# A macaron transformer block on one core: where the first Hadamard stage gets its first batch ready, and where the routed rows of the last two batches are added

## The chip, the cores and the metric

The kernel runs on one core of one Trainium2 chip. The metric is the device time of one execution in microseconds (us). The engines are PE (TensorE), DVE (VectorE), ACT (ScalarE), POOL (GpSimd) and SP (SyncE, which here only issues DMA transfers).

## The reference

The input `x` has 4 batches of 512 tokens with 256 features, all float32. Five layers follow each other, each added to its input:

```
x = x + 0.5 * experts(layernorm(x))          # 8 experts, the best 2 of each token, twice in all
x = x + attention(layernorm(x))              # causal, rotary, 16 heads
x = x + 0.5 * experts(layernorm(x))
x = x + 0.5 * hadamard_ffn(layernorm(x))     # silu(x W1) * (x W3), Walsh-Hadamard transform, W2
x = x + feature_attention(layernorm(x))      # sine and cosine features
x = x + 0.5 * hadamard_ffn(layernorm(x))
```

In the experts layer every token is sent to two experts, and the two results come back weighted by the token's two routing weights. The Hadamard layer's transform is folded into its last weight: `W2` is multiplied with the Hadamard matrix once, ahead of the layer.

## The kernel before

The whole `x` stays in SBUF, as `g.x`: 16 tiles of 128 tokens, 4 tiles to a batch. The program is a chain of stages (`experts_stage` 0, `attention_stage`, `experts_stage` 1, `hadamard_stage` 0, `features_stage`, `hadamard_stage` 1). Each stage is one block in which the five engines run their own hand-written lists in parallel and wait for each other by semaphores. Between two stages stands a barrier of all engines (`Semaphores.clear`, L64 to L66): no engine begins the next stage before all have ended this one and POOL has cleared the stage's semaphores.

float32 products are made of three matmuls of a high and a low part. ACT makes the high part of an operand (a copy to the type float32r) and DVE the low part (the operand less its high part).

**The end of experts stage 1.** The expert units write the results of the routed tokens to the DRAM tensor `made_rows`. Then SP waits until all of it is written and issues eight transfers of 512 KB (L564), for each batch `b` the rows of the first choice and of the second (`r` is 0 or 1). They land in `back`, which has two slots (`b % 2`) in the space of the expert weights `w`: batches 0 and 1 are fetched at once, batches 2 and 3 when their slot has been read. DVE adds them to `g.x` (L1040), one `scalar_tensor_tensor` for each tile and each `r`: 8 instructions for a batch, 32 in all. Meanwhile PE multiplies `W2` with the Hadamard matrix into banks 0 to 3 of PSUM (L726, 128 matmuls), ACT takes its high part (L823), and DVE its low part (L1028), between the adds of batch 1 and of batch 2.

**The start of Hadamard stage 0.** `Norm` is a helper whose methods stand in each engine's list. For a batch, `stats` on DVE takes mean and variance of the 4 tiles (L91, L96); `rstd` on POOL makes the inverse deviation (L119, L122); `normalise` on DVE applies it (L131); `turn` on PE transposes the batch into two banks (L142, 8 transposes); `high` on ACT (L148) and `low` on DVE (L153) split it. Only then can PE start on batch 0.

**The units of Hadamard stage 0.** There are 32 units `n`, 8 (`c`) for each batch `b`. `first(n)` on PE (L1978) is 12 matmuls of 512 columns; ACT's sigmoid (L2031), DVE's `gate` (L2076) and `product` (L2083), ACT's `high` (L2037) and DVE's `low` (L2088) make the hidden part, and `second(n)` on PE (L1990) is 12 matmuls of 256 columns with `W2`. PE runs two units ahead: its list is first(n + 2), second(n). DVE's list in unit `n` is gate(n + 1), low(n), product(n + 1), and then, where the unit has one, a piece of other work: with c = 0 the adding of the batch before to `g.x` (L2095), with c = 1 the statistics of the next batch, with c = 2 its normalising, with c = 4 its split. With c = 3, 5, 6 and 7 there is none.

## Time and profile before

| what | value |
|---|---|
| time, median of 3 runs | 1222.45 us (1217.13 to 1224.24) |
| the profiled execution: its own time | 1228.02 us |
| the profiled execution: its span, from the first to the last instruction | 1226.3 us |
| PE busy, share of the span | 84% |
| DVE busy, share of the span | 60% |
| mean granted TensorE clock | 0.899 of full speed |

The profiled execution is one execution, and its time of 1228.02 us lies 5.6 us above the median. The span leaves out 1.7 us around the instructions. All durations are read from this execution. The rows of a timeline give the start in us from the beginning of the span, the duration in us, the engine, the line of the kernel and the instruction, how many of them are merged in the row (x), and in square brackets how long the engine was idle before and what released it.

### The profile page before, as it was taken

How to read it: one execution, taken by the hardware profiler on the slowest of the kernel's cores; microseconds unless marked ns; L12 is line 12 of the kernel's file. 1: busy time of each engine (PE TensorE's matmuls, PEld its weight loads, DVE VectorE, ACT ScalarE, POOL GpSimd, SP SyncE). 2: the span in 40 equal slices, each digit the busy share in tenths (PEclk: the TensorE clock that was granted, in tenths of full speed). 3: DMA queues.
4: the chain of work that ended last, by engine and by line, in shares of the span. 5: the costliest groups of instructions: out<-in, count | busy, mean ns of one | idle time of the engine just before them, and what ended most of it. 6: DMA issues, size and time to landing. Idle time of an engine off the chain costs nothing. (4 is left out here: it accounts for less than half of the span.)

```text
span 1226.3 us, 18054 instructions
## 1 busy us (share of the span) xinstructions
PE 1024.6 (84%) x6181; PEld 833.7 (68%) x6181; DVE 736.9 (60%) x1754; ACT 463.2 (38%) x806; POOL 438.6 (36%) x474
## 2 busy tenths in 40 slices
PE   4459996469999999952889893999988998789997
PEld 3348775346566665542678782888878988678886
DVE  5754342786777878537344326565657777656553
ACT  3314332226666765514233320322334443222222
POOL 2036664335363622202365630000109889400000
PEclk9579999667999998875899996999997999999999
DMA  9043222400000001118352233000010030000000
GB/s 338 8 159 100 82 82 79 135 1 1 2 1 19 1 18 35 36 34 328 92 201 82 79 117 112 1 1 1 1 69 1 1 69 1 1 1 18 18 12 24
DMA packets 36878, 72.34 MB, mean 59 GB/s; under 512 B 8180, under 2 KB 25654, under 8 KB 36536
## 3 DMA queue, kind: packets, MB, share of 16 engines
q1 hardware_dynamic: 29112, 50.21, 12.3%
q0 software_dynamic: 7680, 20.98, 5.2%
q8 instruction: 54, 0.88, 0.3%
q14 instruction: 32, 0.26, 0.1%
HBM read 47.04 MB, written 24.13 MB: 58 GB/s over the span
## 5 line engine op out<-in xcount | busy, mean ns | idle before, releaser
L1978 PE MATMUL ps<-xt,w 128*128 128x512 f32 x768 | 192.9, 402 | 5.6 <-PEq L66 3.2
L1978 PEld LDWEIGHTS ps<-xt,w 128*128 128x128 f32 x768 | 143.4, 193 | 35.8 <-DVE xt L153 6.2
L1680 DVE CUSTOM_DVE_ANT_0 ps<-ps,att_mask 128x128 f32<-128x128 f32 (+3 forms) x256 | 119.2, 517 | 39.2 <-PE ps L1295 39.0
L680 PE MATMUL ps<-moe_w,moe_narrow_xb 128*128 x480 | 127.8, 402 | 0.0
L119 POOL TENSOR_TENSOR var_eps<-bn,eps 128x4 f32<-128x4 f32 x24 | 5.2, 217 | 319.8 <-DVE bn L96 292.4
L2076 DVE TENSOR_TENSOR had_gated<-ps,had_sig 128x512 f32<-128x512 f32 x64 | 44.3, 692 | 119.8 <-ACT had_sig L2031 119.8
L590 POOL DMA_INDIRECT moe_xs<-xn_rows,moe_index x80 | 80.6, 1008 | 97.4 <-DVE moe_index L962 52.5
L596 POOL DMA_INDIRECT made_rows<-moe_units_made,moe_index x80 | 81.6, 1020 | 92.8 <-ACT moe_units_made L800 76.9
L981 DVE TENSOR_TENSOR moe_narrow_xb<-ps,moe_narrow_xb 128x512 fp32r<-128x512 f32 x40 | 27.7, 692 | 140.7 <-ACT moe_narrow_xb L782 94.7
L2031 ACT ACTIVATE had_sig<-ps 128x512 f32<-128x512 f32 x64 | 38.2, 597 | 186.4 <-PE ps L1978 186.4
L680 PEld LDWEIGHTS ps<-moe_w,moe_narrow_xb 128*128 128x128 f32 x480 | 92.2, 192 | 19.6
L1546 ACT ACTIVATE att_early_probs<-ps 128x384 f32<-128x384 f32 (+1 forms) x192 | 90.7, 527 | 28.7 <-PE ps L1310 27.7
L1990 PE MATMUL ps<-w,had_yhi 128*128 128x256 f32 x512 | 94.6, 283 | 1.8 <-DVE had_ylo L2088 1.8
L1197 POOL TENSOR_SCALAR_AFFINE_SELECT att_early_probs<-att_early_probs 128x256 f32<-128x256 f32 x128 | 53.6, 432 | 116.5 <-ACT att_early_probs L1546 116.4
L1990 PEld LDWEIGHTS ps<-w,had_yhi 128*128 128x128 f32 x512 | 83.4, 190 | 7.8 <-DVE had_ylo L2088 2.6
L782 ACT ACTIVATE moe_narrow_xb<-ps 128x512 fp32r<-128x512 f32 x40 | 23.9, 598 | 143.5 <-PE ps L664 125.7
L1295 PE MATMUL ps<-att_kt,att_q 48*128 48x256 f32 (+3 forms) x256 | 66.8, 424 | 11.0 <-DVE att_q_stack L1680 8.3
L1990 PE MATMUL ps<-w,had_ylo 128*128 128x256 f32 x256 | 72.4, 283 | 0.0
L2210 POOL TENSOR_TENSOR fea_inv_norm<-fea_norm,neg_half 128x24 f32<-128x24 f32 x16 | 66.7, 4172 | 11.3 <-DVE fea_norm L2437 11.1
L2290 PE MATMUL ps<-fea_wv_prod,ident 128*128 128x256 f32 x256 | 63.3, 405 | 7.4 <-DVE fea_wv_prod L2479 7.4
L706 PE MATMUL ps<-moe_w,moe_units_yb 128*128 x480 | 69.4, 284 | 0.0
L706 PEld LDWEIGHTS ps<-moe_w,moe_units_yb 128*128 128x128 f32 x480 | 63.5, 192 | 0.1
(274 smaller groups left out, 2230.0 us busy)
## 6 DMA issues: line engine op xcount, KB each, us to landing
moe_w<-in_moe SPq DMA_DIRECT2D x16, 768.0 KB, 8.5
back<-made_rows SPq DMA_DIRECT2D x8, 512.0 KB, 5.4
x<-x_turned SPq DMA_DIRECT2D x8, 512.0 KB, 7.6
moe_w<-made_rows SPq DMA_DIRECT2D x8, 512.0 KB, 4.7
low_weights<-moe_w SPq DMA_DIRECT2D x4, 768.0 KB
moe_w<-low_weights SPq DMA_DIRECT2D x4, 768.0 KB, 16.7
x<-in_x SPq DMA_DIRECT2D x4, 512.0 KB, 5.1
xn_rows<-moe_wide_xn SPq DMA_DIRECT2D x4, 512.0 KB, 9.2
```

Of the source, the lines that this page charges most:

```text
L590: nc.gpsimd.indirect_dma_start(out=xs[:, j % 2, i, :], out_offset=None, in_=g.xn_dram[:, :], in_offset=at(0, 2 * j + i)).then_inc(gathered ...
L596: nc.gpsimd.indirect_dma_start(out=g.made_dram[:, :], out_offset=at(1, 2 * j + i), in_=made[:, j % 2, i, :], in_offset=None) \
L680: last = nc.tensor.matmul(h_bank(j, i), xb[a][:, j % 2, i, k, :], weight(c), start=False, stop=(k == KC - 1 and c == 1))
L706: last = nc.tensor.matmul(O_BANK[:, i * D:(i + 1) * D], yb[a][:, j % 2, i, c, :], weight(q), start=False, stop=(c == IC - 1 and q == 1), s ...
L1197: last = nc.gpsimd.affine_select(block, block, [[0, 2], [1, P]], ALU.is_ge, 0.0, base=0, channel_multiplier=-1)
L1295: last = nc.tensor.matmul(g.ps[:, a, col:col + n], q1[at, w % 2, i * P:n], kt[at, w % 4, 0:n], start=True, stop=True)
L1546: nc.scalar.activation(probs[:, w % 3, a, at:at + n], g.ps[:, 2 + a, 0:n], ACT.Exp, scale=HD ** -0.5).then_inc(exp_done, 1)
L1680: last = nc.vector.tensor_tensor_reduce(g.ps[:, a, col:col + n], g.ps[:, a, col:col + n], mask[:, SEQ - n:SEQ], -1.0, 3.0e38, ALU.add, ALU ...
L1978: last = nc.tensor.matmul(g.ps[:, bank(n, half), :], w[a][:, k, c * P:(c + 1) * P], xt[low][:, b % 2, k, :], start=(k == 0 and q == 0), st ...
L1990: last = nc.tensor.matmul(o, a[:, n % 4, at], g.w2[w][:, c, :], start=(c == 0 and q == 0 and i % 2 == 0), stop=(c == HC - 1 and q == 2), s ...
L2210: nc.gpsimd.tensor_tensor(inv_norm[:, t % 4, :], norm2[:, t % 4, :], g.neg_half[:, 0:QKH], ALU.pow) \
L2290: last = nc.tensor.matmul(g.ps[:, 5 + t % 2, 0:D], g.ident[:, :], wv_prod[:, t % 2, k, :, :].rearrange("p h d -> p (h d)"), start=(k == 0) ...
```

## The change

Batch 0 of Hadamard stage 0 is added, normalised, transposed and split at the end of experts stage 1, ahead of the barrier. In detail:

- `f.xn`, `f.xt` and `f.back` get fixed places in SBUF where the expert weights were; `f.back` has three slots instead of two, and it stays alive into the Hadamard stage. SP so issues six transfers at once (batches 0, 1 and 2) and those of batch 3 after batch 0 has been added.
- DVE adds batches 0 and 1 at the end of the experts stage. Batches 2 and 3 are added within the Hadamard units, four instructions each after the product of the units (b, c) = (0, 3), (0, 5), (0, 7) and (1, 3).
- `stats`, `rstd`, `normalise`, `turn`, `high` and `low` of batch 0 stand in the experts stage (`f.first_norm`). The transposes go to banks 0 and 1, and the product of `W2` and the Hadamard matrix goes to banks 4 to 7 instead of 0 to 3.
- The low part of `W2` is made by DVE at the start of the Hadamard stage, and PE waits for it (`f.w2_low`) ahead of second(0).
- The statistics of the next batch wait until that batch has been added (`f.combined`).

```diff
-            experts_stage(nc, g, ins, 0, x_dram)
+            experts_stage(nc, g, ins, 0, x_dram, None)
...
+        f = Shared()
+        f.base = nc.sbuf_base
+        f.xn = nc.alloc_sbuf_tensor_at("xn", [P, 2, BT, D], F32, offset=f.base)
+        f.xt = [nc.alloc_sbuf_tensor_at(f"xt{q}", [P, 2, KC, SEQ], F32R, offset=f.base + (q + 1) * 8192) for q in range(2)]
+        f.back = nc.alloc_sbuf_tensor_at("back1", [P, 3, 2, BT, D], F32, offset=f.base + 42 * 1024)
+        f.back_here = [sem(f"back1_here{s}") for s in range(3)]
+        f.combined, f.w2_low = sem("combined1"), sem("w2_low")
+        f.first_norm = Norm(nc, sem, g, "had0_norm", 2, f.xn)
+        experts_stage(nc, g, ins, 1, None, f)
...
+def add_rows(nc, g, f, dve, b, r):
+
+    if r == 0:
+        dve.wait_ge(f.back_here[b % 3], 32 * (b // 3 + 1))
+    else:
+        dve.wait_ge(f.combined, 2 * b + 1)
+    for i in range(BT):
+        t = b * BT + i
+        last = nc.vector.scalar_tensor_tensor(out=g.x[:, t, :], in0=f.back[:, b % 3, r, i, :],
+                                              scalar=g.route[:, r, t:t + 1], in1=g.x[:, t, :],
+                                              op0=ALU.mult, op1=ALU.add)
+    last.then_inc(f.combined, 1)
...
# experts stage 1, SP
-                if b >= 2:
-                    sp.wait_ge(combined, 2 * (b - 1))
+                if b >= 3:
+                    sp.wait_ge(f.combined, 2 * (b - 2))
# POOL
+            if which == 1:
+                f.first_norm.rstd(pool, 0)
# PE
                 for o in range(HC):
+                    if o == HC - 2:
+                        pe.wait_ge(out_done, PAIRS)
...
-                            last = nc.tensor.matmul(g.ps[:, o // 2, (o % 2) * D:(o % 2 + 1) * D], had_r[:, odd, :],
+                            last = nc.tensor.matmul(g.ps[:, 4 + o // 2, (o % 2) * D:(o % 2 + 1) * D], had_r[:, odd, :],
...
+                f.first_norm.turn(pe, 0, 0)
# ACT
+                f.first_norm.high(act, 0, 0, f.xt[0][:, 0, :, :])
# DVE
-            for b in range(BATCH if which == 1 else 0):
...
+                add_rows(nc, g, f, dve, 0, 0)
+                add_rows(nc, g, f, dve, 0, 1)
+                dve.wait_ge(f.combined, 2)
+                f.first_norm.stats(dve, 0, x_block(0))
+                add_rows(nc, g, f, dve, 1, 0)
+                f.first_norm.normalise(dve, 0, x_block(0))
+                add_rows(nc, g, f, dve, 1, 1)
+                f.first_norm.low(dve, 0, 0, f.xt[0][:, 0, :, :], f.xt[1][:, 0, :, :])
+                dve.wait_ge(w2_hi, 1)
...
# Hadamard stage
+        LATE = {(0, 3): (2, 0), (0, 5): (2, 1), (0, 7): (3, 0), (1, 3): (3, 1)}
...
+                if n == 0 and which == 0:
+                    pe.wait_ge(f.w2_low, 1)
...
-                norm.stats(dve, 0, x_block(0))
-                norm.normalise(dve, 0, x_block(0))
-                norm.low(dve, 0, pair(0), xt[0][:, 0, :, :], xt[1][:, 0, :, :])
+                nc.vector.scalar_tensor_tensor(
+                    out=g.w2[1][:, :, :].rearrange("p a n -> p (a n)"),
+                    in0=g.ps[:, 4:8, :].rearrange("p a n -> p (a n)"), scalar=HID ** -0.5,
+                    in1=f32(g.w2[0][:, :, :]).rearrange("p a n -> p (a n)"), op0=ALU.mult, op1=ALU.subtract) \
+                    .then_inc(f.w2_low, 1)
...
+                if which == 0 and (b, c) in LATE:
+                    add_rows(nc, g, f, dve, *LATE[b, c])
                 if c == 1 and b + 1 < BATCH:
+                    if which == 0:
+                        dve.wait_ge(f.combined, 2 * b + 4)
                     norm.stats(dve, b + 1, x_block(b + 1))
```

The first place is DVE's list from the low part of `W3` (L1024 before, L1048 now) to the first gate of the Hadamard stage (L2076 before, L2094 now); the two branches between are the end of one stage and the start of the next. The instructions of before:

```order
L1024 TENSOR_TENSOR w_1_8891<-moe_w_raw,w_0_8890 128x2048
L1040 SCALAR_TENSOR_TENSOR x<-moe_w,moe_route_back,x 128x256 x16
L1028 SCALAR_TENSOR_TENSOR w_1_8893<-ps,w_0_8892 128x2048
L1040 SCALAR_TENSOR_TENSOR x<-moe_w,moe_route_back,x 128x256 x16
L373 UNCONDITIONAL_BRANCH
L2069 UNCONDITIONAL_BRANCH
L91 BN_STATS bn<-x 128x6 x4
L96 BN_AGGR bn<-bn 128x2 x4
L131 TENSOR_SCALAR xn<-x,bn,rstd 128x256 x4
L153 TENSOR_TENSOR xt<-ps,xt 128x1024
L2076 TENSOR_TENSOR had_gated<-ps,had_sig 128x512
```

And the same stretch of the change, in which L387 is the add of the routed rows:

```order
L1048 TENSOR_TENSOR w_1_8891<-moe_w_raw,w_0_8890 128x2048
L387 SCALAR_TENSOR_TENSOR x<-back_8897,route,x 128x256 x8
L94 BN_STATS bn<-x 128x6 x4
L99 BN_AGGR bn<-bn 128x2 x4
L387 SCALAR_TENSOR_TENSOR x<-back_8897,route,x 128x256 x4
L134 TENSOR_SCALAR xn<-x,bn,rstd 128x256 x4
L387 SCALAR_TENSOR_TENSOR x<-back_8897,route,x 128x256 x4
L156 TENSOR_TENSOR xt_8896<-ps,xt_8895 128x1024
L396 UNCONDITIONAL_BRANCH
L2087 UNCONDITIONAL_BRANCH
L2119 SCALAR_TENSOR_TENSOR w_1_8893<-ps,w_0_8892 128x2048
L2094 TENSOR_TENSOR had_gated<-ps,had_sig 128x512
```

Statistics, normalising and split of batch 0 have moved from behind the barrier to ahead of it, 16 of the 32 adds are gone from this stretch, and the low part of `W2` (L1028, now L2119) has moved behind the barrier.

The second place is DVE's list in the units n = 2 to 5 of the change, from the normalising of batch 1 on (L2094 is the gate, L2106 the low part, L2101 the product):

```order
L134 TENSOR_SCALAR xn<-x,bn,rstd 128x256 x4
L2094 TENSOR_TENSOR had_gated<-ps,had_sig 128x512
L2106 TENSOR_TENSOR had_ylo<-had_y,had_yhi 128x512
L2101 TENSOR_TENSOR had_y<-ps,had_gated 128x512
L387 SCALAR_TENSOR_TENSOR x<-back_8897,route,x 128x256 x4
L2094 TENSOR_TENSOR had_gated<-ps,had_sig 128x512
L2106 TENSOR_TENSOR had_ylo<-had_y,had_yhi 128x512
L2101 TENSOR_TENSOR had_y<-ps,had_gated 128x512
L156 TENSOR_TENSOR xt_8896<-ps,xt_8895 128x1024
```

The four adds stand between the product of one unit and the gate of the next, where before stood nothing; the same holds for the three other places.

The third place is PE's list from the last matmuls of `W2` (L748) to the first of the Hadamard stage (L1998):

```order
L748 MATMUL ps<-moe_wide_part_8910,moe_units_had_r 128x256 x8
L748 MATMUL ps<-moe_wide_part_8911,moe_units_had_r 128x256 x8
L145 MATMUL ps<-ident,xn 128x128 x8
L396 UNCONDITIONAL_BRANCH
L1981 UNCONDITIONAL_BRANCH
L1998 MATMUL ps<-xt_8895,w_0 128x512
```

The eight transposes of batch 0 (L145; before, L142 stood behind the two branches) now end PE's list of the experts stage, so that the first matmul after the barrier is one of `first(0)`.

## Rows read from the trace of the kernel before

**Rows 1.** The page: busy time by engine, share of the span, instructions.
```profile
PE 1024.6 (84%) x6181; PEld 833.7 (68%) x6181; DVE 736.9 (60%) x1754; ACT 463.2 (38%) x806; POOL 438.6 (36%) x474
```

**Rows 2.** Timeline of all engines, 724 to 773 us.
```profile
724.33 15.51 PE L726 MATMUL ps<-moe_wide_part,moe_units_had_r 128*128 128x256 f32 x128
...
736.55 6.67 DVE L1040 SCALAR_TENSOR_TENSOR x<-moe_w,moe_route_back,x 128x256 f32<-128x256 f32 x16 [7.28 <-DMA moe_w<-made_rows]
739.88 1.88 ACT L823 ACTIVATE w<-ps 128x2048 fp32r<-128x2048 f32 x1 [12.94 <-PE ps L726]
743.14 2.28 DVE L1028 SCALAR_TENSOR_TENSOR w<-ps,w 128x2048 fp32r<-128x2048 f32 x1
745.34 6.66 DVE L1040 SCALAR_TENSOR_TENSOR x<-moe_w,moe_route_back,x 128x256 f32<-128x256 f32 x16
...
753.23 1.41 DVE L91 BATCH_NORM_STATS2 bn<-x 128x6 f32<-128x256 f32 x4 [1.23 <-PEq L66]
...
754.75 0.38 DVE L96 BATCH_NORM_AGGREGATE bn<-bn 128x2 f32<-128x6 f32 x4
...
755.49 1.05 POOL L122 TENSOR_TENSOR rstd<-var_eps,neg_half 128x4 f32<-128x4 f32 x1
...
756.57 1.39 DVE L131 TENSOR_SCALAR xn<-x,bn,rstd 128x256 f32<-128x256 f32 x4 [1.44 <-POOL rstd L122]
...
758.02 1.97 PE L142 MATMUL ps<-ident,xn 128*128 128x128 f32 x8 [18.18 <-DVE xn L131]
...
760.02 1.02 ACT L148 ACTIVATE xt<-ps 128x1024 fp32r<-128x1024 f32 x1 [18.27 <-PE ps L142]
...
761.08 1.23 DVE L153 TENSOR_TENSOR xt<-ps,xt 128x1024 fp32r<-128x1024 f32 x1 [3.12 <-ACT xt L148]
...
762.36 10.70 PE L1978 MATMUL ps<-xt,w 128*128 128x512 f32 x36 [2.37 <-DVE xt L153]
```

**Rows 3.** Line L66, 750 to 754 us: the barrier's release of PE.
```profile
L66 PEldq EVENT_SEMAPHORE  x1: 51/51/51, 753.1 to 753.1; - x1
```

**Rows 4.** Timeline of DVE, 782 to 798 us: gates behind units 3 and 5.
```profile
787.27 0.69 DVE L2076 TENSOR_TENSOR had_gated<-ps,had_sig 128x512 f32<-128x512 f32 x1 [3.20 <-ACT had_sig L2031]
...
795.72 0.69 DVE L2076 TENSOR_TENSOR had_gated<-ps,had_sig 128x512 f32<-128x512 f32 x1 [2.33 <-ACT had_sig L2031]
```

**Rows 5.** Windows: us, busy time of each engine, PEclk (granted clock), DMA share, GB/s.
```profile
742.90:758.00 15.10, 0.00 (x0) 0.00 (x0) 12.21 (x30) 0.00 (x0) 2.47 (x8) 0.50 0.53 180
762.36:766.90 4.54, 4.54 (x11) 3.57 (x12) 0.00 (x0) 0.00 (x0) 0.00 (x0) 0.50 0.03 1
773.00:860.00 87.00, 87.00 (x506) 76.46 (x505) 52.81 (x107) 25.43 (x43) 4.37 (x7) 1.00 0.00 1
```

**Rows 6.** DMA issues of 729.0 to 729.5, 729.5 to 730.0 and 730.6 to 731.2 us.
```profile
moe_w<-made_rows SPq DMA_DIRECT2D x1, 512.0 KB, 4.2
...
moe_w<-made_rows SPq DMA_DIRECT2D x1, 512.0 KB, 7.0
...
moe_w<-made_rows SPq DMA_DIRECT2D x1, 512.0 KB, 8.5
```

**Rows 7.** One window inside that burst, columns as in rows 5.
```profile
734.00:735.00 1.00, 1.00 (x10) 1.00 (x9) 0.00 (x0) 0.00 (x0) 0.00 (x0) 1.00 1.02 397
```

**Rows 8.** Timeline of DVE and POOL, 812 to 814 and 882 to 888 us.
```profile
812.43 1.04 POOL L122 TENSOR_TENSOR rstd<-var_eps,neg_half 128x4 f32<-128x4 f32 x1
...
813.20 0.68 DVE L2088 TENSOR_TENSOR had_ylo<-had_y,had_yhi 128x512 fp32r<-128x512 f32 x1
...
882.67 2.75 POOL L1959 TENSOR_TENSOR lqkv<-had_lqkv_raw,lqkv 128x1024 fp32r<-128x1024 f32 x1
...
883.67 3.86 DVE L131 TENSOR_SCALAR xn<-x,bn,rstd 128x256 f32<-128x256 f32 x4
```

**Rows 9.** Windows at the start of Hadamard stage 1, columns as in rows 5.
```profile
1076.29:1079.50 3.21, 0.00 (x0) 0.03 (x1) 1.67 (x2) 1.06 (x2) 0.00 (x0) 1.00 0.00 0
...
1080.94:1084.15 3.21, 3.21 (x9) 2.44 (x8) 0.00 (x0) 0.31 (x1) 0.00 (x0) 0.50 0.00 0
```

More of the change, by code:

```diff
@@ L69, with __init__ @@
 class Norm:
-    def __init__(self, nc, sem, g, tag, slots):
-        self.nc, self.g, self.slots = nc, g, slots
+    def __init__(self, nc, sem, g, tag, slots, rows=None):
+        self.nc, self.g, self.slots, self.rows = nc, g, slots, rows
         s = lambda n: sem(f"{tag}_{n}")
@@ L83, in __init__, with xn @@
         self.lo_done = s("lo_done")
+    def xn(self):
+        return self.g.xn if self.rows is None else self.rows
     def slot(self, b):
@@ L111, in normalise_tiles @@
         for i in tiles:
-            last = nc.vector.tensor_scalar(g.xn[:, q, i, :], x_block(i), g.bn2[:, q, i, 0:1],
+            last = nc.vector.tensor_scalar(self.xn()[:, q, i, :], x_block(i), g.bn2[:, q, i, 0:1],
                                            g.rstd[:, q, i:i + 1], ALU.subtract, ALU.mult)
@@ L130, in normalise @@
         for i in range(BT):
-            last = nc.vector.tensor_scalar(g.xn[:, q, i, :], x_block(i), g.bn2[:, q, i, 0:1],
+            last = nc.vector.tensor_scalar(self.xn()[:, q, i, :], x_block(i), g.bn2[:, q, i, 0:1],
                                            g.rstd[:, q, i:i + 1], ALU.subtract, ALU.mult)
@@ L283, in program @@
         g.lout = upper(ctx, "lout", [P, KC, D])
-        f = Shared()
-        f.xn = sb("xn", [P, 2, BT, D])
-        f.xt = [sb(f"xt{q}", [P, 2, KC, SEQ], F32R) for q in range(2)]
+        sb("front_space", [P, 24 * 256])
         f.bias = sb("bias", [P, 3])
@@ L367, in constants, with experts_stage @@
     nc.gpsimd.tensor_tensor(g.row_e[:, :], g.row_e[:, :], g.row[:, :], ALU.add).then_inc(done, 1)
-def experts_stage(nc, g, ins, which, x_dram):
+def add_rows(nc, g, f, dve, b, r):
[9 more added lines that the diff above has]
+    last.then_inc(f.combined, 1)
+def experts_stage(nc, g, ins, which, x_dram, f):
     with ExitStack() as ctx:
@@ L382, in experts_stage @@
             route_rows = sb("route_rows", [2 * TILES, P])
[L383 removed]
+            route_back = g.route
         b1_all = sb("b1_all", [P, E, 2 * IC])
@@ L397, in experts_stage @@
         xs = sb("xs", [P, 2, 2, D])
-        back = f32(w[0][:, :, :]).rearrange("p e n -> p (e n)")[:, 0:4 * BT * D] \
-            .rearrange("p (s r t d) -> p s r t d", s=2, r=2, t=BT)
         units = Region(nc, ctx, f"{tag}_units", 20480)
@@ L461, in experts_stage @@
         yhi_done, ylo_done, o_ready, out_done = sem("yhi_done"), sem("ylo_done"), sem("o_ready"), sem("out_done")
-        back_here = [sem(f"back_here{s}") for s in range(2)]
-        combined = sem("combined")
         if which == 0:
@@ L563, in _ @@
                     mine = by_sixteens(rows)[:, b * BT:(b + 1) * BT, :]
-                    sp.dma_start(back[:, b % 2, r, :, :], mine).then_inc(back_here[b % 2], 16)
+                    sp.dma_start(f.back[:, b % 3, r, :, :], mine).then_inc(f.back_here[b % 3], 16)
         @block.gpsimd
@@ L1024, in _ @@
                 nc.vector.tensor_tensor(g.w3[1][:, :, :], w3_raw[:, :, :], f32(g.w3[0][:, :, :]), ALU.subtract)
-            for b in range(BATCH if which == 1 else 0):
-                if b == 2:
-                    dve.wait_ge(w2_hi, 1)
-                    nc.vector.scalar_tensor_tensor(
-                        out=flat(g.w2[1][:, :, :]), in0=flat(g.ps[:, 0:4, :]), scalar=HID ** -0.5,
-                        in1=f32(flat(g.w2[0][:, :, :])), op0=ALU.mult, op1=ALU.subtract)
-                dve.wait_ge(back_here[b % 2], 32 * (b // 2 + 1))
-                dve.wait_ge(x_here[b], 16)
-                if b == 0:
-                    dve.wait_ge(route_here, 16)
-                for r in range(2):
-                    if r:
-                        dve.wait_ge(combined, 2 * b + 1)
-                    for i in range(BT):
-                        t = b * BT + i
-                        last = nc.vector.scalar_tensor_tensor(
-                            out=g.x[:, t, :], in0=back[:, b % 2, r, i, :], scalar=route_back[:, r, t:t + 1],
-                            in1=g.x[:, t, :], op0=ALU.mult, op1=ALU.add)
-                    last.then_inc(combined, 1)
+                for b in range(BATCH):
+                    dve.wait_ge(x_here[b], 16)
+                dve.wait_ge(route_here, 16)
+                add_rows(nc, g, f, dve, 0, 0)
[7 more added lines that the diff above has]
+                dve.wait_ge(w2_hi, 1)
 def attention_stage(nc, g, ins):
@@ L1891, in hadamard_stage @@
         yhi_done, ylo_done, second_done, x_added = sem("yhi_done"), sem("ylo_done"), sem("second_done"), sem("x_added")
-        norm = Norm(nc, sem, g, "norm", 2) if which == 0 else f.next_norm
+        norm = f.first_norm if which == 0 else f.next_norm
         BLOCKS = P // HD
         UNITS = HC * BATCH
+        LATE = {(0, 3): (2, 0), (0, 5): (2, 1), (0, 7): (3, 0), (1, 3): (3, 1)}
         x_block = x_of(g)
@@ L2006, in turn_tables @@
                 last.then_inc(f.tables_ps, 1)
-            if which == 0:
-                turn(0)
             first(0)
@@ L2037, in high @@
                 nc.scalar.activation(yhi[:, n % 4, :], y[:, n % 2, :], ACT.Copy).then_inc(yhi_done, 1)
-            if which == 0:
-                norm.high(act, 0, pair(0), xt[0][:, 0, :, :])
             sigmoid(0)
@@ L2114, in _ @@
                     add(b - 1)
+                if which == 0 and (b, c) in LATE:
+                    add_rows(nc, g, f, dve, *LATE[b, c])
                 if c == 1 and b + 1 < BATCH:
+                    if which == 0:
+                        dve.wait_ge(f.combined, 2 * b + 4)
                     norm.stats(dve, b + 1, x_block(b + 1))
```

9 lines of the change are left out of this document (4 added, 5 removed).

## The prediction

> **What bounds the kernel now.** I read the page first: PE is busy 84% of the span, more than any other engine [rows 1]. So a stretch in which PE stands still is where time can be won. The timeline shows one between the two stages [rows 2]. PE's last matmul of the `W2` product ends at 724.33 + 15.51 = 739.84 us, and its first matmul of the Hadamard stage starts at 762.36 us: 22.5 us in which PE does eight transposes (1.97 us) and nothing else. In the same rows the reader can follow what PE waits for. DVE waits until 736.55 us for the routed rows, adds 16 tiles (6.67 us), makes the low part of `W2` (2.28 us), adds 16 more (6.66 us) and ends at 745.34 + 6.66 = 752.00 us. Then come the barrier (DVE starts again at 753.23 us), statistics (to 754.75 + 0.38 = 755.13 us), POOL's inverse deviation, normalising (to 757.96 us), transposes, high part and low part (to 762.31 us), one after the other. The chain begins with the landing of the rows, and it is DVE's from there to 757.96 us, but for the barrier and POOL.
>
> In the units behind it PE is the bound. From 773 to 860 us it is busy 87.00 of 87.00 us [rows 5], and DVE waits in every unit for the sigmoid, 2.33 us ahead of a gate behind a unit without other work, and 3.20 us behind the unit c = 3, in which PE transposes [rows 4]. The two gates there stand two units apart, so a unit lasts (795.72 - 787.27) / 2 = 4.22 us.
>
> **The change part by part.** I take the distance from DVE's first add to PE's first matmul, 762.36 - 736.55 = 25.81 us, and build it again in the new order. One add takes 6.67 / 16 = 0.417 us.
>
> 1. Adds of batch 0, eight: 3.33 us.
> 2. Statistics, from the first to the end of the last, 755.13 - 753.23 = 1.90 us.
> 3. Adds of batch 1, first choice, four: 1.67 us. Before, DVE waited from 755.13 to 756.57 us, 1.44 us, for POOL [rows 2]; that wait now lies under these adds. POOL has issued its last scatter long before, so nothing is ahead of it in its queue.
> 4. Normalising: 1.39 us.
> 5. From its end to the end of the low part, 762.31 - 757.96 = 4.35 us, the same three steps on the same engines. The other four adds of batch 1 (1.67 us) lie under the transposes, since the low part waits for ACT anyway. ACT is free: its high part of `W2` ends at 739.88 + 1.88 = 741.76 us. PE stood at half clock for these transposes before (0.50 from 742.90 to 758.00 us [rows 5]); in the new order they come some 5 us after PE's last matmul, and I take them at half clock again.
> 6. The barrier: from DVE's end to PE's release, 753.1 + 0.05 - 752.00 = 1.15 us [rows 3]. The first matmul needs nothing else then.
>
> The sum is 3.33 + 1.90 + 1.67 + 1.39 + 4.35 + 1.15 = 13.79 us, against 25.81 us: **12.0 us less**. It splits into 16 adds gone from the stretch and four under the transposes (20 x 0.417 = 8.3 us), the low part of `W2` (745.34 - 743.14 = 2.2 us as its part of DVE's time), and POOL's 1.4 us.
>
> What was moved must lie somewhere. The low part of `W2` (2.28 us) now opens DVE's list behind the barrier. Its cover is `first(0)`: the first gate needs PE's twelve matmuls, and `second(0)`, which waits for it, came only behind the 36 matmuls of 10.70 us [rows 2]. Without that cover it would cost 2.28 us. The 16 adds of batches 2 and 3 come in four pieces of 4 x 0.417 = 1.67 us. Behind unit 3, and behind unit 11 in the same position, DVE had 3.20 us free; behind units 5 and 7 it had 2.33 us [rows 4]. So 1.5 and 0.7 us are left over, the gates are not late, and I cost the adds at nothing. If the gaps were not free they would cost up to 4 x 1.67 = 6.7 us. The statistics of batches 2 and 3 wait for adds that stand several units ahead in DVE's own list: nothing.
>
> The transfers: SP now issues six at once. In the burst of four, the first landed after 4.2 us, the second, which batch 0 also needs, after 7.0 us and the last after 8.5 us [rows 6]. They landed in their order, so two more behind them should not delay batch 0: nothing. The bound from the other side is that all share the bandwidth evenly; then two more transfers, 1.05 MB at 397 GB/s [rows 7], make batch 0 late by 2.6 us. Batch 3 is issued when batch 0 is added, as batch 2 was, and needed behind unit 7, over 40 us later. The wait of PE for the last expert output stands ahead of the last quarter of the `W2` product, long after that output: nothing.
>
> The clock: before, PE ran the first 4.54 us behind the wait at half clock [rows 5]. In the new order it has been idle for 3.5 us after the transposes and is at half clock already, so I take the same 4.54 us again. Between nothing gained and half of it, 2.3 us, I choose nothing, since the row nearest to it had eight transposes 2.4 us ahead of it as well.
>
> DVE against POOL: POOL can hold DVE. While POOL ran one `tensor_tensor` of 2.75 us from 882.67 us, four normalisations took 3.86 us [rows 8], where they otherwise take 1.39 us [rows 2]. In the new order the inverse deviation falls on the adds of batch 1. But for this pair the nearest row says nothing happens: the inverse deviation ran from 812.43 to 813.47 us, and a DVE instruction with two inputs from SBUF, as an add has, started at 813.20 us and took its usual 0.68 us [rows 8]. I take nothing, and the bound is POOL's whole part, 756.54 - 755.13 = 1.4 us. The Trainium skill says otherwise (SBUF — State Buffer, section "Who interferes with whom"): a DVE instruction with two SBUF inputs contends with a GpSimd instruction that reads SBUF, and whoever comes second is blocked for the whole of the other. By it the adds and POOL's part would follow one another, and the gain would be 10.6 us.
>
> From the profiled execution's own time of 1228.02 us that leaves 1216.0 us. This execution lies 5.6 us above the median of the runs, 1222.45 us; in the same proportion the median goes to 1222.45 x 1216.0 / 1228.02 = **1210.5 us**.
>
> **The rivals.**
> - *POOL and DVE block each other* over the adds of batch 1. For it speaks the 3.86 us, against it the 0.68 us [rows 8]. It gives 1210.5 + 1.4 = 1211.9 us. Chance 0.10.
> - *Six transfers share the bandwidth* and batch 0 is late. Against it speaks the order of landing [rows 6], for it that the second took 2.8 us longer than the first. 1210.5 + 2.6 = 1213.1 us. Chance 0.10. By the Trainium skill (DMA: Bandwidth & Descriptors, section "Queues, rings and completion order") each DMA engine takes the descriptors of one queue in ring order, which would leave batch 0 where it is.
> - *The late adds reach PE*, because a product or a gate comes late and the two units of lead are used up. Against it speak 0.7 us left in the tightest gap. Wholly exposed they cost 6.7 us: 1217.2 us; half of them 1213.9 us. Chance 0.12.
> - *Slower: PE's clock stays low.* PE enters the stage at half clock, and a unit of 4.22 us then takes up to twice as long. The gain is used up when the half clock holds for 12.0 / 4.22 = 2.8 units longer than before, and the kernel is slower by over 0.5% from 4.3 units on: 1228.6 us or more. Against it: after 15 us of idleness the full clock came back within 4.54 us [rows 5], and after 3.21 us of idleness at the start of the other Hadamard stage half clock held 3.21 us [rows 9]. Chance 0.02.
>
> **How the numbers follow.** The forecast has a chance of 0.62, and 0.04 is left for what I don't see. 1210.5 us is the likeliest. Its own range is 1208 (the half clock saved) to 1213 us (a transfer late). The three runs of before lie from 5.3 us under to 1.8 us over their median, so a median of few runs can be off by some 3 us: I go down to 1205 and, to take in the late adds, up to 1217 us. Within 0.5% (about what a measurement of this kernel can tell from no change) would be above 1216.3 us: there stand half of the late adds' case and little else, 0.07. Slower by over 0.5% is the clock's case, 0.02. Faster: 0.91.
>
> **What would show it.** In the profile of the changed kernel: PE's gap between the `W2` product and the Hadamard stage should be 10.5 us instead of 22.5, with the transposes some 5 us into it; the normalising should start within 0.1 us of the last of four adds (if 1.4 us later, it is POOL); the first add should again come about 7.3 us after the low part of `W3` (if 2.6 us more, the transfers share); the gates behind the late adds should still be released by the sigmoid, with 1.5 and 0.7 us of idleness; and PE should be busy without a break from the first unit on, at full clock after some 4.5 us. The prediction is wrong if PE's first matmul starts later than 752 us, if gates are released by DVE's own adds, or if the low clock lasts longer.

## The result and the profile after

| kernel | median of its runs | runs | ratio to the kernel before, with its interval |
|---|---|---|---|
| before | 1221.38 us (1217.1 to 1224.72) | 6 | |
| changed | 1202.14 us (1198.86 to 1209.8) | 6 | 0.9875 (0.9845 to 0.9906) |

The kernel became faster, by 1.2%. The forecast's ratio was 1210.5 / 1222.45 = 0.990, which lies inside the interval. The profiled execution of the change took 1209.8 us, 18.2 us less than that of before. Only part of this is the change's, and the profile tells which.

The timeline of all engines from the end of experts stage 1 on, in the changed kernel (columns as in rows 2; here and below, `...` stands where rows are left out):

```profile
713.74 13.48 PE L748 MATMUL ps<-moe_wide_part,moe_units_had_r 128*128 128x256 f32 x111
...
716.56 10.98 SPq L582 DMA_DIRECT2D back<-made_rows  x8
723.33 3.38 DVE L387 SCALAR_TENSOR_TENSOR x<-back,route,x 128x256 f32<-128x256 f32 x8 [6.70 <-DMA back<-made_rows]
726.75 1.41 DVE L94 BATCH_NORM_STATS2 bn<-x 128x6 f32<-128x256 f32 x4
...
728.55 1.64 DVE L387 SCALAR_TENSOR_TENSOR x<-back,route,x 128x256 f32<-128x256 f32 x4
...
729.14 1.17 POOL L125 TENSOR_TENSOR rstd<-var_eps,neg_half 128x4 f32<-128x4 f32 x1
730.34 1.38 DVE L134 TENSOR_SCALAR xn<-x,bn,rstd 128x256 f32<-128x256 f32 x4 [0.15 <-POOL rstd L125]
731.64 1.67 DVE L387 SCALAR_TENSOR_TENSOR x<-back,route,x 128x256 f32<-128x256 f32 x4
731.78 1.97 PE L145 MATMUL ps<-ident,xn 128*128 128x128 f32 x8 [4.56 <-DVE xn L134]
733.79 1.02 ACT L151 ACTIVATE xt<-ps 128x1024 fp32r<-128x1024 f32 x1 [4.65 <-PE ps L145]
734.84 1.22 DVE L156 TENSOR_TENSOR xt<-ps,xt 128x1024 fp32r<-128x1024 f32 x1 [1.53 <-ACT xt L151]
...
738.40 11.08 PE L1998 MATMUL ps<-xt,w 128*128 128x512 f32 x36 [4.65 <-PEq L66]
738.41 2.29 DVE L2119 SCALAR_TENSOR_TENSOR w<-ps,w 128x2048 fp32r<-128x2048 f32 x1 [2.35 <-PEq L66]
```

From DVE's first add to PE's first matmul of the Hadamard stage, which I call the seam from here on, it is 738.40 - 723.33 = 15.07 us, against 25.81 us before [rows 2]: 10.7 us less, where the forecast had 12.0. Step by step, forecast and read:

| step | forecast | read |
|---|---|---|
| adds of batch 0 | 3.33 | 726.75 - 723.33 = 3.42 |
| statistics | 1.90 | 728.55 - 726.75 = 1.80 |
| four adds of batch 1 | 1.67 | 1.64, and 0.15 waiting for POOL |
| normalising | 1.39 | 1.38 |
| from there to the end of the low part | 4.35 | 736.06 - 731.72 = 4.34 |
| barrier | 1.15 | 738.40 - 736.06 = 2.34 |

Every step but the last is right within 0.15 us. (The forecast's 1.15 us ends with PE's release by the barrier; in this profile the first matmul starts 0.05 us behind that release.) Of the barrier, the view of one line shows POOL's part (L396 is the end of the stage's block; columns: count, shortest/median/longest ns, first and last start; the last start of each row is the one in this seam):

```profile
L396 DVEq DRAIN  x2: 799/916/1033, 196.4 to 735.1; - x2
...
L396 POOLq DRAIN  x2: 7821/8450/9078, 201.9 to 729.1; - x2
...
L396 PEldq EVENT_SEMAPHORE  x2: 51/51/51, 211.1 to 737.1; - x2
```

and the same line of the kernel before (L373 there):

```profile
L373 DVEq DRAIN  x2: 799/1250/1702, 202.0 to 750.4; - x2
...
L373 POOLq DRAIN  x2: 9077/9082/9088, 207.5 to 725.2; - x2
```

A drain is the instruction with which an engine's queue makes sure at a stage's end that all its work is done. DVE's ends at 735.1 + 1.03 = 736.1 us, but POOL's, begun at 729.1 us, takes 7.82 us, to 736.9 us, and only then is the barrier passed. Before, POOL's drain took 9.08 us from 725.2 to 734.3 us, and DVE was the last, at 752.1 us. In both kernels POOL's drain ends 6.6 us behind POOL's last instruction: before, behind the last scatter, which ended at 727.65 us; in the change, behind the inverse deviation, which ended at 730.31 us and stands near the end of the stage.

The units. The timeline of DVE behind units 3 and 5 (answers to rows 4):

```profile
760.39 1.66 DVE L387 SCALAR_TENSOR_TENSOR x<-back,route,x 128x256 f32<-128x256 f32 x4
763.69 0.69 DVE L2094 TENSOR_TENSOR had_gated<-ps,had_sig 128x512 f32<-128x512 f32 x1 [1.63 <-ACT had_sig L2051]
...
769.72 1.66 DVE L387 SCALAR_TENSOR_TENSOR x<-back,route,x 128x256 f32<-128x256 f32 x4
772.14 0.69 DVE L2094 TENSOR_TENSOR had_gated<-ps,had_sig 128x512 f32<-128x512 f32 x1 [0.76 <-ACT had_sig L2051]
```

The gates are still released by the sigmoid, with 1.63 and 0.76 us of idleness left (forecast: 1.5 and 0.7). From the first matmul to the end of the stage (the release behind the next barrier) it is 146.6 us, before 146.4 us. The granted clock (windows, columns as in rows 5):

```profile
727.20:730.30 3.10, 0.02 (x1) 0.00 (x0) 2.89 (x11) 1.88 (x1) 1.50 (x2) 0.98 0.86 299
730.30:738.40 8.10, 1.97 (x8) 1.59 (x9) 4.19 (x9) 1.02 (x1) 0.04 (x2) 0.50 0.04 18
738.40:742.90 4.50, 4.50 (x11) 3.53 (x12) 2.29 (x1) 0.00 (x0) 1.12 (x6) 0.50 0.78 245
742.90:749.00 6.10, 6.10 (x26) 4.94 (x25) 3.03 (x5) 1.72 (x3) 0.00 (x0) 0.92 0.08 15
```

PE starts the stage at half clock (1.2 GHz). The 0.92 over the next 6.10 us leaves (1 - 0.92) x 6.10 x 2 = 1.0 us more at half clock, so full clock (2.4 GHz) is back after some 5.5 us, where the forecast took 4.54 us [rows 5]. The first 36 matmuls took 11.08 us, before 10.70 us.

**Where the other 7.5 us of the two profiled executions are.** The barrier rows of each profile give the length of every stage. Experts stage 0 took 212.1 us instead of 217.8, experts stage 1 up to the first add 174.7 us instead of 182.0, the features stage 176.1 us instead of 170.6; attention, the units of Hadamard stage 0 and Hadamard stage 1 differ by 0.3 us at most. Together: 5.7 + 7.3 + 10.7 - 5.5 = 18.2 us, of which 10.7 us is the seam. The code of the other three is the same in both kernels, but for the places of some buffers and one wait of PE in experts stage 1. What they depend on is the question of the repeats below.

### The profile page after: what moved, and what is told of

Its sections match the earlier page's. It is cut to its first block and busy times, and to the rows that moved or that the text cites. A ratio compares the mean times of both kernels' runs of the same rounds, so it can differ in the third digit from the quotient of the medians.

```text
span 1208.1 us, 18055 instructions
## 1 busy us (share of the span) xinstructions
PE 1027.2 (85%) x6181; PEld 838.5 (69%) x6181; DVE 734.9 (61%) x1754; ACT 463.0 (38%) x806; POOL 437.2 (36%) x474
## 5 line engine op out<-in xcount | busy, mean ns | idle before, releaser
L1998 PE MATMUL ps<-xt,w 128*128 128x512 f32 x768 | 193.1, 402 | 7.9 <-PEq L66 7.9
L1998 PEld LDWEIGHTS ps<-xt,w 128*128 128x128 f32 x768 | 143.7, 193 | 38.0 <-issue 5.0
L2094 DVE TENSOR_TENSOR had_gated<-ps,had_sig 128x512 f32<-128x512 f32 x64 | 44.2, 691 | 111.5 <-ACT had_sig L2051 111.5
L2314 PE MATMUL ps<-fea_wv_prod,ident 128*128 128x256 f32 x256 | 60.0, 390 | 9.1 <-DVE fea_wv_prod L2503 9.1
```

The costliest lines, as they stand in the source:

```text
L1998: last = nc.tensor.matmul(g.ps[:, bank(n, half), :], w[a][:, k, c * P:(c + 1) * P], xt[low][:, b % 2, k, :], start=(k == 0 and q == 0), st ...
L2314: last = nc.tensor.matmul(g.ps[:, 5 + t % 2, 0:D], g.ident[:, :], wv_prod[:, t % 2, k, :, :].rearrange("p h d -> p (h d)"), start=(k == 0) ...
```

## The experiments

**Theory A**: the change acts at the seam alone, through what it takes off the chain there, and the late adds cost nothing. **Theory B**: it does something more (the other 7.5 us). For the missing 1.2 us at the seam, **theory P**: POOL's drain is long because of the indirect transfers that POOL issued earlier and never drained, and its end moves back when POOL gets an instruction late; **theory Q**: 6 to 7 us behind the last instruction is what a drain of POOL takes in any case.

**1. Both kernels again**, unchanged, on one chip.

> The kernel before, unchanged, once more. Between the two profiled executions so far, stages with the same code differed: experts stage 0 took 217.8 us in one and 212.1 us in the other, the units of experts stage 1 some 7 us less, the features stage 170.6 and 176.2 us. Theory A (these differences belong to the execution, not to the change): this profile differs from the first one of before by several us in these stages, while the distance from the first routed add to the first matmul of the Hadamard stage is again 25.8 us within 0.2 us. Theory B (they come with the change): the stages take 217.8, 336.7 and 170.6 us within 1 us again. The ratio to before is 1.000 within 0.004 under both.

> The changed kernel, unchanged, once more. Theory A (only the seam between the stages gives time, the rest varies by execution): first routed add to first matmul 15.1 us within 0.2 us, the other stages anywhere between the two profiles so far, and a ratio of (1221.4 - 10.7) / 1221.4 = 0.991 within 0.003. Theory B (the change also shortens the experts stages): experts stage 0 again some 212 us, and a ratio of 0.984 to 0.988.

Measured: before 1217.72 us (10 runs), ratio 0.9996 (0.9959 to 1.0033); the change 1208.89 us (6 runs), ratio 0.9886 (0.9848 to 0.9925). Seams 25.80 and 15.07 us. Experts stage 0 took 211.9 and 212.8 us, experts stage 1 to the first add 175.3 and 176.0 us. So in these two profiles the experts stages have the same lengths within 1 us, and the 13.0 us by which they differed in the first pair are not the change's.

**2. The early preparation without the late adds.** The adds of batches 2 and 3 go back to the end of the experts stage, behind the low part of batch 0. The low part of `W2` stays behind the barrier, as in the change.

```diff
+                for b in (2, 3):
+                    for r in range(2):
+                        add_rows(nc, g, f, dve, b, r)
...
-        LATE = {(0, 3): (2, 0), (0, 5): (2, 1), (0, 7): (3, 0), (1, 3): (3, 1)}
+        LATE = {}
```

> Batch 0 is prepared ahead of the barrier as in the change, but batches 2 and 3 are also added there, behind the low part of batch 0. The 16 adds (6.67 us) stand on DVE at the end of the stage, and POOL's drain is over by then: first routed add to first matmul 15.07 + 6.67 - (2.31 - 1.15) = 20.6 us, that is 5.2 us less than before and 5.5 more than the change. If the late adds of the change were in truth partly exposed in the units, the units from first matmul to the stage's end would here be shorter than the 146.5 us of the changed kernel; I expect 146.2 to 146.5 us.

Measured: 1216.18 us (9 runs), ratio 0.9957 (0.9914 to 0.9999); seam 20.83 us, 5.0 us less than before. The 16 adds (6.66 us) stand ahead of the barrier again and cost 20.83 - 15.07 = 5.8 us: they also cover POOL's drain. DVE ends 1.52 us ahead of PE's first matmul here. Of the 5.0 us, 2.2 us belong to the low part of `W2`, which this kernel has off the chain too. From the first matmul to the end of the stage it took 146.8 us, not less than in the change (146.1 to 146.6 us in its three profiles), so the late adds were not partly exposed there.

**3. The late adds alone**, with the low part of `W2` behind the barrier; all six steps of batch 0's preparation go back to the Hadamard stage.

```diff
-                f.first_norm.rstd(pool, 0)
...
-                f.first_norm.turn(pe, 0, 0)
...
-                f.first_norm.high(act, 0, 0, f.xt[0][:, 0, :, :])
...
-                f.first_norm.stats(dve, 0, x_block(0))
...
-                f.first_norm.normalise(dve, 0, x_block(0))
...
-                f.first_norm.low(dve, 0, 0, f.xt[0][:, 0, :, :], f.xt[1][:, 0, :, :])
```

> Batches 2 and 3 are added within the units and the low part of W2 is made behind the barrier as in the change, but batch 0 is normalised, transposed and split behind the barrier as before. First routed add to first matmul: 6.67 (16 adds) + 1.2 (barrier, POOL's drain long over) + 1.90 + 1.44 + 1.39 + 4.35 = 17.0 us, 8.8 us less than before and 1.9 more than the change. So most of the gain would be the work taken out of DVE's list, little the place of the barrier. If the place of the barrier mattered more, this would be above 18 us.

Measured: 1208.09 us (4 runs), ratio 0.9886 (0.9831 to 0.9941); seam 16.98 us, 8.8 us less than before. The timeline of this kernel:

```profile
726.90 6.67 DVE L387 SCALAR_TENSOR_TENSOR x<-back,route,x 128x256 f32<-128x256 f32 x16 [6.58 <-DMA back<-made_rows]
...
738.10 1.38 DVE L134 TENSOR_SCALAR xn<-x,bn,rstd 128x256 f32<-128x256 f32 x4 [1.44 <-POOL rstd L125]
739.41 2.28 DVE L2118 SCALAR_TENSOR_TENSOR w<-ps,w 128x2048 fp32r<-128x2048 f32 x1
...
743.88 10.21 PE L1991 MATMUL ps<-xt,w 128*128 128x512 f32 x36 [2.37 <-DVE xt L156]
```

The low part of `W2` lies under the transposes here, and POOL's 1.44 us are back. So most of the gain needs none of the early preparation: taking 16 adds and the low part of `W2` off the chain is worth 8.8 us. The preparation adds 16.98 - 15.07 = 1.9 us to that. The 5.0 us of (2) and these 8.8 us both hold the 2.2 us of `W2`'s low part, so they don't add up to 10.7 us; and with the late adds gone from the chain, POOL's drain takes back part of what the preparation gives. The ratio of this kernel, 0.9886, is that of the change in (1): the totals don't show the 1.9 us, the seams do.

**4. POOL drained early** (P against Q): a drain in POOL's idle time, ahead of the inverse deviation.

```diff
             if which == 1:
+                nc.gpsimd.drain()
                 f.first_norm.rstd(pool, 0)
```

> The changed kernel with one more instruction: POOL drains right behind its last scatter, while it waits for the statistics anyway (13.7 us idle). In the changed kernel POOL's drain at the end of the stage ends 6.6 us behind the inverse deviation and 0.87 us behind DVE's last instruction, so it is what holds the barrier. Theory P (the 6.6 us belong to the indirect transfers not yet drained): with the drain ahead, the one at the end is short, DVE ends the stage, the barrier takes 1.2 instead of 2.3 us, and first routed add to first matmul is 14.0 to 14.2 us. Theory Q (any POOL work late in this stage costs 6.6 us at its end): 15.1 us as in the change, or more.

Measured: seam 14.40 us (forecast: 14.0 to 14.2); a single run of 1219.8 us, so its total says nothing. The new drain (L625), in the view of its line:

```profile
L625 POOLq DRAIN  x1: 9079/9079/9079, 730.2 to 730.2; - x1
```

the one at the end, in the view of that line:

```profile
L396 POOLq DRAIN  x2: 1272/5180/9088, 208.0 to 746.4; - x2
```

and the timeline up to the first matmul:

```profile
752.16 1.22 DVE L156 TENSOR_TENSOR xt<-ps,xt 128x1024 fp32r<-128x1024 f32 x1 [1.53 <-ACT xt L151]
...
755.04 2.47 PE L1999 MATMUL ps<-xt,w 128*128 128x512 f32 x5 [3.98 <-PEq L66]
```

The 9.08 us are now spent at 730.2 us, where POOL has nothing to do, and they too end 6.6 us behind the last scatter (to 732.63 us); the drain at the end takes 1.27 us instead of 7.82, and DVE is the last at the barrier again. P holds, Q falls: the long drain belongs to something that one drain settles. (The 1.27 us hold the inverse deviation itself: the drain's record begins at 746.4 us, when the 1.17 us of that instruction begin, and ends at 747.7 us, as they do within 0.1 us.) That the something is the indirect transfers fits: in Hadamard stage 0 of the kernel before, which has none, POOL's last instruction ended at 885.38 + 1.35 = 886.7 us and its drain, of 5.12 us from 881.7 us, at 886.8 us. But no run took the transfers away, so it is argued. The seam gets 0.67 us shorter. The barrier's remaining 755.04 - 753.38 = 1.66 us is 0.5 us more than the 1.15 us that I had read off the kernel before. The views of the barrier's own lines show where, first before:

```profile
L65 POOLq EVENT_SEMAPHORE_RANGE_CLEAR  x1: 437/437/437, 752.5 to 752.5; - x1
...
L66 POOLq EVENT_SEMAPHORE  x2: 17/17/17, 753.0 to 753.1; - x2
```

and in the kernel with POOL drained:

```profile
L65 POOLq EVENT_SEMAPHORE_RANGE_CLEAR  x1: 417/417/417, 753.8 to 753.8; - x1
...
L66 POOLq EVENT_SEMAPHORE  x2: 17/17/17, 754.8 to 754.9; - x2
```

Before, POOL passed the barrier on 753.0 - 752.9 = 0.1 us after it had cleared the semaphores; here it took 754.8 - 754.2 = 0.6 us. In the change it took 0.4 us, and in (3), where POOL has no instruction behind its last scatter either, 0.1 us as before. Why POOL is slower there no run isolates.

**5. All 16 late adds in one gap**, that behind unit 5, where DVE has 2.33 us free [rows 4]: the rival of the late adds, made to happen.

```diff
-        LATE = {(0, 3): (2, 0), (0, 5): (2, 1), (0, 7): (3, 0), (1, 3): (3, 1)}
+        LATE = {(0, 5): ((2, 0), (2, 1), (3, 0), (3, 1))}
```

> The changed kernel, but all 16 late adds in one place, behind unit 5: 6.67 us in a gap of 2.33 us, so the next gate is 4.3 us late. The low part behind it was ready 2.1 us before PE wanted it and the product 2.9 us before, so PE should stand still for some 2.2 us once, and first matmul to the end of the stage should be 148.5 instead of 146.4 us. If the lead of PE doesn't count (a late gate stops PE at once), it is 150.7 us; if DVE's time there is free whatever is put in, 146.4 us.

Measured, in a single run of 1223.09 us: seam 15.08 us, from the first matmul to the stage's end 150.1 us instead of 146.4: 3.7 us more, where 2.1 us was expected. Its timeline of PE:

```profile
787.72 2.94 PE L1998 MATMUL ps<-xt,w 128*128 128x512 f32 x12
792.63 0.80 PE L2012 MATMUL ps<-w,had_yhi 128*128 128x256 f32 x2 [1.97 <-DVE had_ylo L2106]
```

and windows at the same place (columns as in rows 5):

```profile
790.66:792.63 1.97, 0.00 (x1) 0.00 (x0) 1.97 (x5) 0.60 (x1) 0.00 (x0) 1.00 0.00 0
792.63:795.36 2.73, 2.73 (x12) 2.73 (x13) 2.44 (x4) 0.63 (x1) 0.00 (x0) 0.50 0.01 3
795.36:798.47 3.11, 3.11 (x14) 2.54 (x13) 0.00 (x0) 0.00 (x0) 0.00 (x0) 0.89 0.00 0
```

The adds take 6.67 us, 4.3 us more than the gap; the lead of two units hides 2.4 us of it, and PE stands still for 1.97 us. After that its clock is at half for 2.73 us and at 0.89 for 3.11 us more, which costs 2.73 x 0.50 + 3.11 x 0.11 = 1.7 us. 1.97 + 1.7 = 3.7 us: a wait of PE costs nearly twice its length here. The length of the wait was forecast well (2.2 us); the cost in clock was left out of the forecast.

**6. PE kept busy** with 32 matmuls of 256 columns between the `W2` product and the transposes and 20 behind them, whose results nobody reads, so that it might arrive at full clock.

```diff
+                def keep_busy(count):
+                    for _ in range(count):
+                        nc.tensor.matmul(g.ps[:, 3, 0:D], had_r[:, 0, :], part[0][:, 0, :], start=True, stop=True)
+                keep_busy(32)
                 f.first_norm.turn(pe, 0, 0)
+                keep_busy(20)
```

> The changed kernel with idle work on PE in the seam: 32 matmuls of 256 columns into an unused bank ahead of the transposes of batch 0 and 20 behind them; nothing reads them. In the changed kernel PE is idle for 4.6 us, transposes at half clock (1.97 us), is idle again for 4.6 us and runs the first 4.5 us of the stage at half clock. If the idleness is what costs the clock, the transposes take 1.04 us and the first 36 matmuls about 8.5 instead of 11.1 us: first add to first matmul 14.3 us (less 0.2 to 0.9 if the drain holds), and first matmul to the end of the stage 144.0 instead of 146.4 us. If the clock falls regardless, all stays as in the change.

Measured: 1224.62 us (10 runs; before on this chip 1233.85 us), ratio 0.9929 (0.99 to 0.9958). Seam 15.08 us, unchanged: the transposes took 1.09 us instead of 1.97, but POOL's drain held the barrier all the same. The expected 14.3 us was missed. PE stood still for 3.15 us ahead of its first matmul, and its clock was 0.71 over the first 5.0 us of the stage. From the first matmul to the end it took 145.4 us, 1.0 us less than the change's 146.4 us; but the kernel of (4), without these matmuls, took 145.6 us, because full clock was back after 3.15 us there. So this one profile does not show that the 1.0 us is the edit's.

**7. Both: POOL drained and PE kept busy.**

> Both edits together, POOL's early drain and PE kept busy. Under theory P and with the clock held: first add to first matmul 13.1 to 13.4 us, first matmul to the end of the stage 144.0 us, together 4.0 to 4.5 us less than the change; ratio to before about 0.991 less 0.0035 = 0.988, within 0.004.

Measured: 1222.59 us (6 runs), ratio 0.9884 (0.9841 to 0.9928). Seam 13.58 us and 144.1 us to the end, together 157.7 us; the change has 15.07 + 146.3 = 161.4 us there (146.3 us is the mean of its three profiles). That is 3.7 us less, where 4.0 to 4.5 us was expected. The same kernel was run again with the change beside it (8); its timeline of PE there:

```profile
751.50 1.10 PE L145 MATMUL ps<-ident,xn 128*128 128x128 f32 x8 [0.67 <-DVE xn L134]
752.35 2.63 PE L755 MATMUL ps<-moe_wide_part,moe_units_had_r 128*128 128x256 f32 x20
756.62 8.61 PE L2004 MATMUL ps<-xt,w 128*128 128x512 f32 x36 [1.64 <-PEq L66]
```

and its windows:

```profile
740.00:756.00 16.00, 14.31 (x119) 13.90 (x117) 10.89 (x29) 2.91 (x2) 1.51 (x2) 1.00 0.56 210
756.00:760.00 4.00, 3.38 (x15) 2.80 (x16) 2.29 (x1) 0.33 (x1) 1.15 (x6) 1.00 0.59 192
```

With PE idle for 1.64 us only, the clock stays at full speed (2.4 GHz), and the first 36 matmuls take 8.61 us instead of 11.08.

**8. The change, the drained kernel and the one of (7), side by side** on one chip.

> The changed kernel once more, as the measure for the two kernels beside it. If only the seam is the change's doing (10.7 us of some 1221 us), its ratio to the kernel before is 0.991; if the rest of what the first comparison showed (0.9875) belongs to the change too, 0.987 to 0.988. First add to first matmul 15.07 us.

> The changed kernel with POOL drained ahead of the inverse deviation. Its seam was 14.40 us instead of 15.07 us, so it should lie 0.7 us under the changed kernel, which is less than the comparison can tell: the two medians within 0.3% of each other. A rival would be that the drain delays POOL somewhere else: then over 0.3% above the changed kernel.

> POOL drained and PE kept busy with matmuls whose results nobody reads. From the stage lengths read so far (seam 13.58 us against 15.07 us, first matmul to the stage's end 144.1 us against 146.4 us) it should lie 3.8 us under the changed kernel, a ratio of 0.997 to it, and 0.988 to the kernel before. Rival: the features stage falls into its long pattern more often when PE arrives at full clock, and gives 5 us back: then it lies level with the changed kernel or up to 2 us over it.

Measured, with 1236.5 us for the kernel before: the change 1222.69 us (9 runs), ratio 0.9923 (0.9878 to 0.9968); drained 1218.66 us (12 runs), 0.9883 (0.9847 to 0.9919); both edits 1220.52 us (6 runs), 0.9869 (0.9822 to 0.9916). The three intervals overlap. Their seams were 15.08, 14.40 and 13.58 us as before, so the 3.7 us are there in the stages, but the total does not tell the three kernels apart.

**9. The kernel before a third time**, for its stage lengths.

> The kernel before once more, for its stage lengths. The features stage, whose code is the same in all kernels, has so far lasted 170.4 to 170.7 us in the four profiles in which Hadamard stage 0 took 150 us or more, and in the nine in which it took 144 to 147 us it lasted 168.4 to 170.4 us three times and 175.3 to 178.5 us six times. If a shorter Hadamard stage 0 is what brings the long form, this profile has the short one, 170.5 us; if it comes by execution alone, with a chance of 6 in 13, 175 to 178 us may come here as well. One profile can only speak against the first. First add to first matmul 25.8 us.

Measured, in a single run of 1218.68 us: seam 25.80 us, experts stage 0 212.1 us, features stage 170.5 us.

**What the repeats say of theory B.** The experts stages follow the chip. On the two chips of (1), (2), (3) and of (9) experts stage 0 took 211.9 to 212.8 us in all five profiles, and experts stage 1 to the first add 174.8 to 176.0 us; on the two chips of (4) to (8) it was 216.1 to 222.5 us and 180.7 to 184.5 us in all seven. The first five hold both kernels; the seven are all kernels with the change in it, and that the kernel before is longer there too shows in its medians alone (1233.85 and 1236.5 us against 1218.16 us). On which chips the first pair was profiled isn't on record. The features stage is another matter. It has two lengths, and the windows from its start show the difference, first in the changed kernel:

```profile
884.90:893.90 9.00, 7.28 (x44) 6.37 (x45) 5.90 (x14) 3.10 (x5) 0.21 (x2) 1.00 0.56 235
893.90:917.90 24.00, 24.00 (x104) 22.94 (x104) 6.30 (x16) 6.97 (x9) 18.10 (x6) 0.50 0.00 1
```

and in the same kernel run again:

```profile
892.50:898.50 6.00, 5.94 (x20) 4.75 (x21) 2.31 (x4) 1.37 (x2) 0.00 (x0) 0.72 0.82 344
898.50:919.50 21.00, 17.99 (x142) 16.91 (x140) 12.63 (x29) 9.90 (x15) 16.84 (x7) 1.00 0.01 3
919.50:934.50 15.00, 13.15 (x57) 12.70 (x58) 14.46 (x32) 6.73 (x9) 14.37 (x7) 0.56 0.00 1
```

In the first, half clock comes after 9 us and stays for 24 us; in the second there is a short piece of it in the first 6 us, and the long one comes only after 27 us and covers some 13 of the next 15 us. That makes 176.1 us of one and 168.9 us of the other, of the same instructions. All fourteen profiles are of one or the other kind: six have 24 to 27 us of half clock from 8 to 11 us on (175.3 to 178.5 us), eight have 14 to 17 us of it from 28 to 29 us on (168.3 to 170.7 us). At which clock the stage begins does not tell them apart. The kernel of (6) has half clock in the first 11 us and still the long form:

```profile
897.20:908.20 11.00, 9.41 (x49) 8.07 (x50) 6.08 (x15) 3.38 (x6) 0.78 (x2) 0.84 0.45 191
908.20:932.00 23.80, 23.80 (x101) 22.54 (x100) 6.17 (x16) 7.04 (x9) 17.54 (x6) 0.50 0.00 1
```

and the drained kernel of (8) begins at full clock and has the short one:

```profile
899.70:908.40 8.70, 7.16 (x43) 6.25 (x44) 5.90 (x14) 3.10 (x5) 0.18 (x1) 1.00 0.58 243
...
912.00:929.00 17.00, 14.44 (x111) 13.51 (x110) 10.48 (x18) 8.55 (x12) 15.65 (x6) 1.00 0.00 1
929.00:942.60 13.60, 13.60 (x55) 12.61 (x55) 13.07 (x30) 5.57 (x9) 13.52 (x7) 0.50 0.00 1
```

What decides between the two stays open. The kernels with a Hadamard stage 0 of 150 us or more had the short form in five profiles of five; those with 144 to 147 us had it in three, and the long one in six, among them all three in which PE was kept busy. If this is no chance, a shorter Hadamard stage 0 gives 5 to 8 us back in most executions; the runs here are too few to say so.

## Why the prediction was right

- **The mechanism held, and with it the sum.** Five of the six terms were right within 0.15 us, and (2) and (3), in which one part of the change is taken back at a time, came out at 20.83 and 16.98 us, where sums of such terms had given 20.6 and 17.0 us.
- **The step that was off is the barrier**, the term of 1.15 us, which measured 2.34 us. Of the 1.2 us between them, 0.67 us is POOL's drain, shown by (4). The other 0.5 us is still there in (4): POOL passes the barrier on 0.6 us after it has cleared the semaphores, before 0.1 us. Only 0.05 us of it is that I took the span to PE's release and not to its first matmul. The cause of the slower release stays open. The two parts together are why the gain at the seam is 10.7 and not 12.0 us. I had checked POOL's queue for what stands ahead of the inverse deviation, but not for what stands behind it.
- **POOL's wait under the adds of batch 1** cost 0.15 us. The rival of the blocking is wrong: POOL's two instructions took 0.34 and 1.17 us instead of 0.20 and 1.05, the four adds 1.64 us, where the forecast had 1.67. The rule of the Trainium skill (SBUF — State Buffer, "Who interferes with whom") that the second of such a pair is blocked for the whole of the first isn't seen in this pair.
- **Six transfers at once** delayed nothing: the first add came 723.33 - 716.56 = 6.8 us after SP began to issue, before 736.55 - 729.15 = 7.4 us. The prediction's reading that the four of before "landed in their order" is not quite right. It was made without the third transfer, issued at 730.0 us, whose row in the same view is this:

```profile
moe_w<-made_rows SPq DMA_DIRECT2D x1, 512.0 KB, 6.2
```

It belongs to batch 1 and landed at 736.2 us, while the second, of batch 0, landed at 729.5 + 7.0 = 736.5 us. So the two batches overlapped by 0.4 us, far less than the 2.6 us of even sharing. By the Trainium skill (DMA: Bandwidth & Descriptors, section "Queues, rings and completion order") each DMA engine takes up descriptors in ring order, but completion need not keep that order. The trace fits both: two more transfers behind them cost batch 0 nothing, and the second and third landed in reverse.

- **The late adds** cost nothing in four gaps (146.1 to 146.6 us from the first matmul to the end of the stage in three profiles, 146.1 to 146.4 us in three of before), and (5) shows that this rests on the gaps: in one gap they cost 3.7 us.
- **The clock** came back some 5.5 us after the first matmul where the forecast took 4.54 us; the term was sized by one execution, and in another of the same kernel it was 4.2 us. Half a microsecond at the most hangs on it. The slower rival had nothing to it.
- **The total.** The seam's 10.7 us are 0.9% of 1221 us, a ratio of 0.991. The three comparisons gave 0.9875, 0.9886 and 0.9923; two of the intervals hold 0.991 and the first ends just under it (0.9906). The median of 1202.14 us lies 8.4 us under the forecast and 2.9 us under its range. That the ratio came out close to the forecast (0.9875 against 0.990) is in part luck, since the seam alone gives 0.991. Where those microseconds come from stays open: the profiles show no other stage that the change makes shorter, the medians of one kernel differ by 18 us between the chips here (1218.16 to 1236.5 us), and the six runs behind the median spread over 11 us. The profiled execution is the slowest of the six, with the features stage in its long form; with the short one (168.9 to 170.4 us) it would have taken 1202.6 to 1204.1 us, near the median. That is an estimate, since the other five were not profiled.

## What to carry to other kernels

Before work is moved ahead of a barrier, look at how every engine ends its stage, and not only at the engine that ends last now: here a POOL instruction of 1.2 us brought out a drain that had been hidden, and an early drain in idle time took 0.67 us of it back at the seam, which is too little for the totals to show. Take work off the chain first: moving 16 adds and one split into gaps of the next stage brought 8.8 of the 10.7 us, and preparing the next batch early only 1.9 us more. And size the pieces by the gap that each goes into: in (5) one piece too long made PE wait for 1.97 us, and that cost 3.7 us, 1.7 of them in clock.

## What the runs showed of the hardware

- POOL's drain at the end of a stage with indirect transfers took 9.08 us, and 7.82 us when POOL had an instruction that ended 1.2 us into it; in both cases it ended 6.6 us behind POOL's last instruction. With one drain earlier the last took 1.27 us and ended with that instruction.
- 1.97 us of idleness of PE in the units was followed by half clock for 2.7 us and 0.89 for 3.1 us more. 1.64 us at the barrier left the clock at full, in the kernel that had kept PE busy up to there; after 3.15 us it was 0.71 over the next 5.0 us.
- The features stage, with the same instructions, took 168.3 to 170.7 us or 175.3 to 178.5 us. In the long form PE was busy for 24.00 of 24.00 us and yet at half clock (0.50).
